# Pre-norm layer with linear attention and a mixture of experts: the second layer norm applied by ScalarE, the small norm operations on GpSimd, and all instruction lists remade

## What is computed

```python
x = L0_attn_x                                     # (16, 512, 256) float32
x = x + attention(layernorm(x), Wq, Wk, Wv, Wo)
x = x + experts(layernorm(x), ...)
def layernorm(x): return (x - mean(x)) / sqrt(var(x) + 1e-5)
# attention: q = elu(x Wq.T) + 1, k likewise, v = x Wv.T, 16 heads of 16
#   out_i = q_i . sum_(j<=i) k_j v_j  /  (q_i . sum_(j<=i) k_j + 1e-8), then Wo
# experts: sigmoid router with bias, 4 groups of 2, best 2 groups, top 4 of 8, weights * 2.5
#   sum over chosen e of w_e * (silu(x Wg_e) * (x Wu_e)) Wd_e, plus one shared expert
```

## Time and profile before

| | |
|---|---|
| median of three runs | 1011.97 us |
| profiled execution, own time | 1008.9 us |
| its span | 1007.1 us |
| PE busy | 986.0 us (98%) |
| DVE busy | 876.0 us (87%) |
| POOL busy | 595.9 us (59%) |
| ACT busy | 446.8 us (44%) |
| PE in the chain that ended last | 92% |
| granted TensorE clock | 0.998 of full speed |

### The profile page before, as it was taken

The page is one execution under the profiler, slowest core; times in us unless marked ns, Lnnn a source line. Parts: engine busy times, 40 slices in busy tenths (PEclk is TensorE's granted clock), DMA queues, the critical chain, the costliest instruction groups (busy, mean ns, idle before and its releaser), DMA issues.

```text
span 1007.1 us, 25374 instructions
## 1 busy us (share of the span) xinstructions
PE 986.0 (98%) x10037; PEld 847.2 (84%) x10037; DVE 876.0 (87%) x1832; ACT 446.8 (44%) x780; POOL 595.9 (59%) x470
## 2 busy tenths in 40 slices
PE   7899999999999999999999999999999999999998
PEld 6677888888888888888888888888888888888887
DVE  5898889898998989989898998988989898998564
ACT  7755353444534445354354543445353354532322
POOL 7866656557555574656647454675655647454654
PEclk9999999999999999999999999999999999999999
DMA  7002534336252543424335342453324434241421
GB/s 256 2 2 76 113 74 122 75 105 131 77 130 44 144 98 107 105 75 121 82 106 119 82 123 58 131 113 106 98 75 121 89 106 96 72 110 45 123 74 53
DMA packets 235604, 96.67 MB, mean 96 GB/s; under 512 B 161760, under 2 KB 217696, under 8 KB 235488
## 3 DMA queue, kind: packets, MB, share of 16 engines
q1 hardware_dynamic: 235488, 95.07, 37.0%
...
## 4 chain that ended last, share of the span: by engine, by line
PE 92%; POOL 2%; DVE 2%; issue 1%; DMA 1%; ACT 0%; SPq 0%; DVEq 0%; POOLq 0%; ACTq 0%
PE bank L1044 56%; PE y_bank L1044 21%; PE bank L1180 6%; PE bank L1163 5%; PE bank L1196 2%; POOL wg_lo L737 1%; PE bank L1142 1%; DMA x_in<-in_x 1%; PE bank L1210 1%; POOL h_lo L779 0%; DVE scores L916 0%; DVE stats L796 0%; SPq L551 0%; POOL et L776 0%; DVE den L924 0%
## 5 line engine op out<-in xcount | busy, mean ns | idle before, releaser
L776 POOL TENSOR_TENSOR et<-et,cw_all 128x512 f32<-128x512 f32 x124 | 161.3, 1319 | 137.1 <-DVE et L1018 125.0
L1044 PE MATMUL bank<-xt_hi,wg_hi 128*128 128x512 f32 x576 | 235.0, 408 | 0.3 <-DVE scores L916 0.2
L1044 PE MATMUL bank<-xt_lo,wg_hi 128*128 128x512 f32 x576 | 227.9, 396 | 0.0
L1044 PE MATMUL bank<-xt_hi,wg_lo 128*128 128x512 f32 x576 | 227.9, 396 | 0.0
L779 POOL TENSOR_TENSOR h_lo<-et,h_hi 128x512 fp32r<-128x512 f32 x142 | 181.6, 1305 | 53.1 <-ACT h_hi L725 52.9
L916 DVE TENSOR_TENSOR scores<-bank,cst 128x512 f32<-128x512 f32 x240 | 152.4, 680 | 23.5 <-PE bank L1163 20.8
L1044 PE MATMUL y_bank<-wd_hi,h_hi 128*128 128x256 f32 x576 | 164.5, 286 | 0.0
L1044 PE MATMUL y_bank<-wd_lo,h_hi 128*128 128x256 f32 x576 | 161.3, 280 | 0.0
L1044 PE MATMUL y_bank<-wd_hi,h_lo 128*128 128x256 f32 x576 | 161.2, 280 | 0.0
L725 ACT ACTIVATE h_hi<-et 128x512 fp32r<-128x512 f32 x144 | 86.3, 627 | 147.8 <-POOL et L776 91.7
L716 ACT ACTIVATE et<-bank 128x512 f32<-128x512 f32 x144 | 84.2, 597 | 130.8 <-PE bank L1044 95.3
...
## 6 DMA issues: line engine op xcount, KB each, us to landing
...
```

What stands on the lines that cost most here:

```text
L776: nc.gpsimd.tensor_tensor(et[:, i % ET, :], et[:, i % ET, :], weights, ALU.mult).then_inc(weighed, 1)
L1044: ins = nc.tensor.matmul(dst, l, r, start=first and n == 0, stop=last and n == 2, skip_group_check=shared)
```

## The change

The second norm's `ln2_apply` moves from DVE to ACT, with a shift in place of the subtracted mean. The addition of eps and the sign of the mean move from DVE to POOL, for both norms: `scale_and_shift` issues four small operations where POOL had two (first norm) or one (second norm). The statistics of the two norms have a buffer each. All lists in `FIRST`, `STEP` and `LAST` and the table `BANK` are made anew; matmuls and transfers are the same in number.

The last four pieces of the diff below are from the lists: `STEP` of PE, then of `FIRST` the heads of ACT and SP, then the end of `LAST` of PE.

```diff
-        stats = sb("stats", [P, SUBS, 6])
+        stats1, stats2 = (sb(n, [P, SUBS, 6]) for n in ("stats1", "stats2"))
         mv1, mv2 = (sb(n, [P, SUBS, 2]) for n in ("mv1", "mv2"))
-        minus_mean, veps1, rstd1, shift1 = (sb(n, [P, SUBS]) for n in ("minus_mean", "veps1", "rstd1", "shift1"))
-        veps2, rstd2 = (sb(n, [P, SUBS]) for n in ("veps2", "rstd2"))
+        minus, small, veps1, rstd1, shift1 = (sb(n, [P, SUBS]) for n in ("minus", "small", "veps1", "rstd1", "shift1"))
+        veps2, rstd2, shift2 = (sb(n, [P, SUBS]) for n in ("veps2", "rstd2", "shift2"))
...
+                elif name == "ln2_apply":
+                    act.wait_ge(shift2_ready, SHIFT2["rstd2", 0, b])
+                    wait_at(act, 0, b)
+                    wait_at(act, 1, b)
+                    for s in range(SUBS):
+                        last = nc.scalar.activation(norm2[:, s, :], x_mid[b % 2][:, s, :], ACT.Identity,
+                                                    scale=rstd2[:, s:s + 1], bias=shift2[:, s:s + 1])
+                    last.then_inc(norm2_ready, 1)
...
+            nc.gpsimd.memset(minus[:, :], -1.0).then_inc(zeros_set, 1)
+            nc.gpsimd.memset(small[:, :], LN_EPS).then_inc(zeros_set, 1)
+            pool.wait_ge(zeros_set, 5)
+            def scale_and_shift(mv, veps, rstd, shift, ready, n):
+                nc.gpsimd.tensor_tensor(veps[:, :], mv[:, :, 1], small[:, :], ALU.add).then_inc(ready, 1)
+                nc.gpsimd.tensor_tensor(shift[:, :], mv[:, :, 0], minus[:, :], ALU.mult).then_inc(ready, 1)
+                pool.wait_ge(ready, n + 2)
+                nc.gpsimd.tensor_tensor(rstd[:, :], veps[:, :], power, ALU.pow).then_inc(ready, 1)
+                pool.wait_ge(ready, n + 3)
+                return nc.gpsimd.tensor_tensor(shift[:, :], shift[:, :], rstd[:, :], ALU.mult)
+
             for name, i, b in program("POOL"):
...
-                    nc.gpsimd.tensor_tensor(rstd1[:, :], veps1[:, :], power, ALU.pow).then_inc(rstd1_ready, 1)
-                    pool.wait_ge(rstd1_ready, b + 1)
-                    nc.gpsimd.tensor_tensor(shift1[:, :], minus_mean[:, :], rstd1[:, :], ALU.mult)\
-                        .then_inc(shift_ready, 1)
+                    scale_and_shift(mv1, veps1, rstd1, shift1, rstd1_ready, 3 * b).then_inc(shift_ready, 1)
...
-                    nc.gpsimd.tensor_tensor(rstd2[:, :], veps2[:, :], power, ALU.pow).then_inc(rstd2_ready, 1)
+                    scale_and_shift(mv2, veps2, rstd2, shift2, rstd2_ready, 3 * b).then_inc(shift2_ready, 1)
...
-            def layernorm_stats(src, mv, veps, ready, loaded=None, value=0):
+            def layernorm_stats(src, stats, mv, ready, loaded=None, value=0):
...
-                link(last)
-                nc.vector.tensor_scalar(veps[:, :], mv[:, :, 1], LN_EPS, None, ALU.add).then_inc(ready, 1)
+                last.then_inc(ready, 1)
...
-                    nc.vector.tensor_scalar(minus_mean[:, :], mv1[:, :, 0], -1.0, None, ALU.mult)\
-                        .then_inc(var1_ready, 1)
...
-                    layernorm_stats(x_mid[b % 2], mv2, veps2, var2_ready)
-                elif name == "ln2_apply":
-                    dve.wait_ge(rstd2_ready, RSTD2["rstd2", 0, b])
-                    wait_at(dve, 0, b)
-                    wait_at(dve, 1, b)
-                    for s in range(SUBS):
-                        last = nc.vector.tensor_scalar(norm2[:, s, :], x_mid[b % 2][:, s, :], mv2[:, s, 0:1],
-                                                       rstd2[:, s:s + 1], ALU.subtract, ALU.mult)
-                    last.then_inc(norm2_ready, 1)
+                    wait(dve, var2_ready, VAR2, "ln2_stats", 0, b - 1)
+                    layernorm_stats(x_mid[b % 2], stats2, mv2, var2_ready)
...
-        down.6.3 k.0.0 q.0.0 up.2.2 k.1.0 up.1.2 q.1.0 v.0.0 down.7.3 down.8.3 scores.0.0 up.3.2 v.1.0
+        inter.3.1 inter.2.1 values.3.1 gate.1.2 up.0.2 gate.2.2 k.0.0 q.0.0 q.1.0 k.1.0 up.2.2 up.1.2
+        down.7.3 v.1.0 down.6.3 down.8.3 v.0.0 scores.0.0 gate.5.2 gate.3.2 up.3.2 gate.4.2 down.0.2
...
-        piece.0.0 piece.1.0 piece.2.0 piece.3.0 turn.1.0 turn.0.0 piece.5.0 piece.4.0 k.0.0 q.0.0 k.1.0 piece.6.0 q_split.0.0
+        piece.1.0 piece.4.0 piece.2.0 turn.1.0 turn.0.0 piece.0.0 piece.3.0 piece.5.0 k.0.0 piece.7.0 k.1.0
...
-        load_x.0.0 consts.0.0 piece.0.0 piece.1.0 piece.2.0 piece.3.0 consts.1.0 piece.5.0 piece.4.0 load_x.0.1 piece.7.0 piece.11.0
+        load_x.0.0 consts.0.0 piece.1.0 piece.2.0 piece.4.0 piece.3.0 piece.0.0 piece.5.0 load_x.0.1
...
-        up.7.15 gate.8.15 down.4.15 down.3.15 down.5.15 down.7.15 down.6.15 down.8.15
+        up.5.15 up.7.15 gate.7.15 down.2.15 down.3.15 up.6.15 down.4.15 up.8.15 gate.8.15 down.5.15
+        down.6.15 down.7.15 down.8.15
```

199 lines of the change are left out of this document (99 added, 100 removed).

## The result

The changed kernel takes 1013.4 us (median of 9 runs, 1012.3 to 1015.0) where the kernel before takes 1011.4 (9 runs beside them): ratio 1.0024, 95% interval 1.0013 to 1.0036. It is 2.0 us slower, where 2.5 us faster was forecast; the time is inside the range of the prediction. Its profiled execution has a span of 1012.0 us, against 1007.1 before. The two profiled executions are 4.9 us apart and the medians 2.0: the one of the kernel before, at 1008.9 us, is 2.5 under its median, and the one of the changed kernel, at 1013.9, is 0.5 over. So the traces show where time goes, and how much it is worth is read from medians.

A forecast was written before the change was run, and what follows sets the result against it. TensorE, busy 986.0 of 1007.1 us, was taken to bound the kernel. The scores.0 stall's -3.7 and the opening's +1.2, all else 0, summed to -2.5: 1009.5 us from a median of 1011.97, range 1004 to 1017.

The forecast's parts named there:

- PE's matmuls are the same in both kernels.: Premise for TensorE throughout: unchanged matmuls, so a better order can gain only within its 21 us of idle time.
- Step 1: VectorE loses the second norm's apply and three small operations a step; worth nothing by itself, as nothing waits there.
- Step 2: Repeated steps, ahead of scores.0: TensorE's stall of 0.46 us, 8 times, goes; -3.7 us, bounds 0 and -3.7.
- Step 3: Second norm's chain, wo.1 to gate.0: 20.8 us by GpSimd, 20.3 by memory, both fit TensorE's 21.5; nothing charged.
- Rival D: Slower: gate.0 waits each step after stretched q_lo and late get, 22.3 us, 0.8 late; 1017.3 at 0.6 late; chance 0.20.
- Step 4: Opening: k.0 1.3 us later, more tile-form changes, partly caught up in later waits; +1.2 us, bounds -3 to +3.5.
- The bound of +3.5: Opening's worst case: start 1.3, tile forms 0.8, and 1.4 at the masks.
- Step 5: End: down.8 is fed in time, last adds and stores are the same; 0, at worst +0.6 us.
- the alternation of steps: Repeated steps: the trace after would no longer alternate between 60.4 and 60.9 us.
- clean steps of 60.4: Repeated steps: each would last 60.4 us in the trace after; over 60.7 would make the forecast wrong altogether.
- the 4 allowed: Opening: TensorE's idle time differing by more than 4 us either way would make the forecast wrong altogether.

The follow-up runs named there:

- kernel 2: Changed kernel with the first weight pieces loaded and split in the old order; 1009.4 us, ratio 0.9981 to the kernel before.
- kernel 5: Changed kernel with 96 unused bytes ahead of et, h_hi and h_lo, restoring their old addresses; 1011.6 us, ratio 1.0007 to the kernel before.
- kernel 3: Changed kernel with only the last block's load, GpSimd and TensorE lists reordered; 1013.2 us, ratio 1.0021 to the kernel before.
- kernel 10: Changed kernel with first weight pieces in old order, last block's lists reordered and 96 unused bytes ahead of et, h_hi and h_lo; 1007.5 us.
- 15: Changed kernel with 96 unused bytes between et and h_hi, so only h_hi and h_lo regain their old addresses; 1011.2 us, ratio 0.9998.
- 6: Kernel before, operations and lists untouched, with its buffers at the changed kernel's addresses; 1013.8 us, ratio 1.0033 to the kernel before.
- 4: Changed kernel's code with the kernel before's lists and bank table, only the second norm's normalisation moved to ScalarE; 1019.3 us, ratio 1.0079.
- 8: Changed kernel with the second norm's normalisation back on VectorE, ahead of q_split.1; 1070.6 us, ratio 1.0588 to the kernel before.
- 16: Changed kernel with the second norm's normalisation back on VectorE, behind q_split.1; 1045.1 us, ratio 1.0341 to the kernel before.
- 12: Kernel before with buffers up to the statistics 256 bytes lower, et, h_hi and h_lo at their old addresses; 1010.9 us, ratio 0.9999.
- 11: Changed kernel with the second norm's power computed twice on GpSimd, lengthening its chain; 1029.0 us, ratio 1.0176 to the kernel before.

## Why the prediction was wrong

The sign failed, by two terms: the opening, priced +1.2, cost +4.0, and the place of h_hi and h_lo, which the sum did not have, +1.8. In medians the account closes: from 1011.4, the scores.0 stall and the rest of the step -3.9, the opening +4.0 (kernel 2), the place of h +1.8 (kernel 5), the end +0.2 (kernel 3), gives 1013.5; measured 1013.4. The -3.9 is what is left when the three others are undone (kernel 10, 1007.5), not measured by itself, and by the ratio of kernel 10 to the kernel before beside it, 0.9966, it is -3.4. That it is near the -3.7 of the forecast is therefore support, not proof.

*"PE's matmuls are the same in both kernels."* The premise ahead of the steps, and it failed. They are the same in number and shape, and `down` takes 0.15 us more in each step, shown by 5 and 15, and by 6 the other way round. Nothing in the diff of operations or lists tells it; it hung on two lines that I had read as bookkeeping, the new small buffers and the smaller scratch.

*Step 1, VectorE lighter, worth nothing.* Right for the steps in the old order (4 against 6), incomplete in the new one: there the 1.4 us decide (8, 16).

*Step 2, the stall at scores.0 gone, -3.7.* Right in mechanism. In one and the same place the middle is 4.5 us shorter (731.4 to 726.9), or 5.3 (730.4 to 725.1, kernels 12 and 5), since the old order has 10 and 11 stalls there and not 8. In the two kernels as they stand, the slower `down` hides half or more of it.

*Step 3, the chain 20.8 or 20.3 against 21.5.* The cover is 0.55 us where 0.7 was summed, and the way by memory ends last, not GpSimd's queue: from get to take it needs 4.45 us (607.24 to 611.69), not 3.7. Rival D did not come: no wait for xt_lo in the steps. Its warning was right, as a chain 1.36 us longer cost 15.6 us (11), for the most part at another place than gate.0. Rival D's sum of 22.3 counts the stretched q_lo and the late get, but not the 0.43 of the longer power, which it names with them; with it the sum is 22.8.

*Step 4, the opening +1.2.* The step that failed most. k.0 came 3.4 us later, not 1.3: I had priced piece.4 as 1.06 us of ScalarE's time and not as a wait for its transfer, 2.65 us. And I had left out what follows from idle time on PE, the clock: +2.6 us on 18 matmuls in this trace. The kernel before has 8 filler transposes ahead of k.0 and waits 0.96 us; I counted the fillers (35 in both) and not their place. The bound of +3.5 was too low for the 4.8 of the trace.

*Step 5, the end 0, at worst +0.6.* 1.7 in the trace, from three waits for late splits, products and copies that the sum did not look at; 0.7 of it went with new lists, and 0.2 in the median.

Of the statements on the trace: the alternation of steps is gone, as said; clean steps of 60.4 were to come and are 60.54 (and 60.40 in kernel 5); the opening's idle time grew by 2.5 us, inside the 4 allowed, and its loss in time by more, as a matmul at half clock counts as busy.
